# Graph layer on one core: node ranges of 46, ScalarE loads edge attributes, SyncE fetches part of the source rows

## What is computed

```python
nodes = node_state[edges].reshape(num_edges, -1)      # source's and destination's features: 128
gates = (ssp(edge_state @ We1 + be1) @ We2 + be2) * soft_cutoff(edges_distance)
h = ssp(nodes @ Wn1 + bn1) @ Wn2 + bn2
message_sum = zeros.at[edges[:, 1]].add(h * gates)     # scatter-add by destination
new_state = node_state + (ssp(message_sum @ Ws1 + bs1) @ Ws2 + bs2)
out = layernorm(x + new_state)
```

## Time and profile before

| | us |
|---|---|
| median of 3 runs | 2500.21 (2497.41 to 2500.76) |
| span of the profiled execution, first to last instruction | 1988.8 |
| median less span: what lies around the instructions | 511.4 |
| GpSimd (POOL) busy, 1572 instructions | 1484.7 (75%) |
| TensorE (PE) busy | 1737.7 (87%) |
| ScalarE (ACT) busy | 1532.1 (77%) |
| VectorE (DVE) busy | 1285.6 (65%) |
| mean granted TensorE clock | 0.949 of full speed |

### The profile page before, as it was taken

How to read it: one execution, slowest core, us unless ns; L and a number is a source line. 1 busy time by engine, 2 the same in 40 slices (tenths; PEclk the granted TensorE clock), 3 DMA queues, 4 the chain that set the end, 5 groups by cost and what they waited for, 6 DMA issues and landing times.

```text
span 1988.8 us, 53540 instructions
## 1 busy us (share of the span) xinstructions
PE 1737.7 (87%) x16249; PEld 1328.7 (67%) x16249; DVE 1285.6 (65%) x3512; ACT 1532.1 (77%) x3368; POOL 1484.7 (75%) x1572
## 2 busy tenths in 40 slices
PE   4699999898888988878889988998988898988987
PEld 3577777676666666666666766766666676766666
DVE  4578888666665655555656666666666666666666
ACT  3589999777777777777777788788777787787877
POOL 7777777777777777777777777777777777777773
PEclk7799999999999899999989999899999899999999
DMA  5433333333333333333333333333333233333331
GB/s 122 122 85 98 97 97 97 85 85 76 91 74 73 71 73 70 75 68 71 74 71 74 74 80 74 74 75 78 74 75 75 69 84 75 75 78 75 75 76 38
DMA packets 256432, 157.78 MB, mean 79 GB/s; under 512 B 45401, under 2 KB 227046, under 8 KB 256366
## 3 DMA queue, kind: packets, MB, share of 16 engines
q1 hardware_dynamic: 202652, 104.94, 18.2%
q0 software_dynamic: 50048, 51.35, 15.5%
q10 hardware_dynamic: 3666, 0.68, 0.2%
HBM read 146.94 MB, written 9.87 MB: 79 GB/s over the span
## 4 chain that ended last, share of the span: by engine, by line
POOL 57%; issue 22%; PE 11%; DVE 3%; ACT 2%; SPq 2%; DMA 2%; DVEq 1%; ACTq 1%; POOLq 0%
POOL ga L459 57%; PE ps L623 3%; PE ps L636 3%; PE ps L640 1%; DVE hid L1113 1%; SPq L340 1%; PE ps L585 1%; DMA ga<-in_x_dram,srcT 1%; PE ps L575 1%; DVE hid L1117 1%; PE ps L653 1%; PE ps L662 1%; PE ps L577 0%; DVEq L1139 0%; ACT lg L861 0%
## 5 line engine op out<-in xcount | busy, mean ns | idle before, releaser
L459 POOL DMA_INDIRECT ga<-in_x_dram,srcT x1564 | 1483.7, 949 | 477.6 <-issue 472.4
L852 ACT ACTIVATE lg<-ps,bn1c 128x512 f32<-128x512 f32 x391 | 268.4, 687 | 306.6 <-PE ps L585 267.6
L636 PE MATMUL ps<-wn,hid 128*128 128x64 f32 x3128 | 447.9, 288 | 18.9 <-DVE hid L1117 17.1
L1113 DVE SCALAR_TENSOR_TENSOR hid<-ps,neg_b,lg 128x512 f32<-128x512 f32 x391 | 292.8, 749 | 221.9 <-ACT lg L867 205.2
L636 PEld LDWEIGHTS ps<-wn,hid 128*128 128x128 f32 x3128 | 393.1, 197 | 51.5 <-DVE hid L1117 26.6
L575 PE MATMUL ps<-ident,ea 128*128 128x128 f32 x782 | 173.8, 305 | 198.2 <-DMA ga<-in_x_dram,srcT 135.2
L844 ACT COPY xe<-ps 128x512 f32<-128x512 f32 x391 | 229.9, 588 | 113.3 <-PE ps L577 99.8
L623 PE MATMUL ps<-xe,wn 64*128 64x256 f32 x1564 | 289.8, 449 | 0.0
L1151 DVE TENSOR_TENSOR acc<-acc,ps 64x64 f32 x782 | 168.4, 215 | 163.7 <-issue 157.9
L640 PE MATMUL ps<-we,hid 128*128 128x128 f32 x1564 | 273.1, 299 | 0.0
L575 PEld LDWEIGHTS ps<-ident,ea 128*128 128x128 f32 x782 | 80.0, 143 | 282.1 <-issue 268.8
(11 more groups left out here) (124 smaller groups left out, 1847.9 us busy)
## 6 DMA issues: line engine op xcount, KB each, us to landing
ea<-in_edge_attr_dram SPq DMA_DIRECT2D x195, 256.0 KB
ga<-in_x_dram,srcT POOLq DMA_INDIRECT x1564
bw<-b_tab SPq DMA_DIRECT2D x782, 32.0 KB
relb<-rel_tab SPq DMA_DIRECT2D x196, 64.0 KB
b_tab<-share SPq DMA_DIRECT2D x25, 250.0 KB
out_dram<-xs SPq DMA_DIRECT2D x25, 125.0 KB
xs<-in_x_dram SPq DMA_DIRECT2D x3, 750.0 KB
rows_i<-in_dst_dram SPq DMA_DIRECT2D x1, 768.0 KB
```

The costliest lines, as they stand in the source:

```text
L459: pool.indirect_dma_start(to[:, t % 2, t // 2, :], None, x, bass.IndirectOffsetOnAxis(ap=idx[:, t:t + 1], axis=0)).then_inc(done, 16)
L636: pe.matmul(hg[:, t * D:(t + 1) * D], hid[:, u % 2, t * P:(t + 1) * P], wn2[:, :], start=False, stop=False, skip_group_check=True)
L852: act.activation(lg[:, u % 2, 0:QUAD].rearrange("p (k e) -> p k e", k=2), z[:, :, 0:PAIR], ACT.Abs, bias=bn1c[:, 0:1]).then_inc(n_abs, 1)
L1113: dve.scalar_tensor_tensor(out=hid[:, u % 2, 0:QUAD].rearrange("p (k e) -> p k e", k=2), in0=ps[:, 2 * (u % 2):2 * (u % 2) + 2, 0:PAIR], s ...
```

## The change

1. `W` is 46. The layout in partitions stays at halves of 64 (`HALF`). `bw` loads have 46 rows, the one-hot of the scatter has 4 x 46 columns, its matmuls 46, the adds into `acc` 46.
2. A second table `wb_all` holds the places in bytes, so SyncE needs no arithmetic between reading a place and the `bw` load. ScalarE stores and loads that table at the start.
3. The loads of edge attributes are issued by ScalarE, after the bias refill of every other quad.
4. For 23 quads (32, 48, ..., 384) the last of the four gathers is gone. SyncE loads the 128 source rows of it one by one, each with a DMA of 256 B into `stage`: 16 of them in each two-quad step from 22 quads before (`load_rows`), their addresses read from `row_at`. In the step of four quads before, `hand_rows` copies the 128 rows to the `ga` buffer. GpSimd waits for that copy (`handed`) before its third gather of the quad.
5. `row_at` is filled before SyncE's first step with every second of 256 entries of `src` for 23 quads, 2944 words of 4 bytes on one partition; VectorE multiplies them by 256 after its step 7 (`row_ready`).
6. SyncE's loops are written out.

```diff
-W = 64
+HALF = 64
+W = 46
 RING = 4
 ARING = 16
 EPS = 1e-5
 SHARES = 2
 SOON = 2
 BRING = 8
+
+ROWS0 = 32
+ROWS_EVERY = 16
+ROWS_N = 23
+ROWS_BEFORE = 22
+ROWS_TURN = (16,) * 8
...
+        def issue_ea(eng, q, u):
+
+            if isinstance(q, int) and q == NQ - 1:
+                full = edge_attr[q * QUAD:q * QUAD + PAIR, :].rearrange("(p j) d -> p (j d)", j=2)
+                eng.dma_start(ea[:, u, 0, :], full).then_inc(s_ea[u], 16)
+                part = edge_attr[q * QUAD + PAIR:E, :].rearrange("(p j) d -> p (j d)", j=2)
+                eng.dma_start(ea[0:REMP // 2, u, 1, :], part).then_inc(s_ea[u], 16)
+            else:
+                two = edge_attr[bass.ds(q * QUAD, 2 * QUAD), :]
+                eng.dma_start(ea[:, u:u + 2, :, :].rearrange("p q k c -> p (q k) c"),
+                              two.rearrange("(m p j) d -> p m (j d)", p=P, j=2)).then_inc(s_ea[u], 16)
...
+            def load_rows(q):
+
+                i, turn = divmod(q - (ROWS0 - ROWS_BEFORE), ROWS_EVERY)
+                turn //= 2
+                if not (q >= ROWS0 - ROWS_BEFORE and i < ROWS_N):
+                    return
+                if i == 0 and turn == 0:
+                    sp.wait_ge(row_ready, 1)
+                if i >= 2 and turn == 0:
+                    sp.wait_ge(xe_t, ROW_QUADS[i - 2] + 1)
+                first, n = ROWS_FIRST[turn], ROWS_TURN[turn]
+                _, places = nc.values_load_multi_w_load_instructions(
+                    row_at[:, i * P + first:i * P + first + n], engines=(mybir.EngineType.SP,), min_val=0,
+                    max_val=(N - 1) * D * 4, skip_runtime_bounds_check_because=IN_X)
+                for r, place in enumerate(places):
+                    sp.dma_start(stage[first + r:first + r + 1, i % 2, :].bitcast(U8),
+                                 x_bytes[bass.ds(place, D * 4)].rearrange("(r b) -> r b", r=1)).then_inc(s_stage[i % 2], 16)
+
+            def hand_rows(q):
+
+                i = (q - (ROWS0 - 4)) // ROWS_EVERY
+                if (q - (ROWS0 - 4)) % ROWS_EVERY or not 0 <= i < ROWS_N:
+                    return
+                quad = ROW_QUADS[i]
+                sp.wait_ge(s_stage[i % 2], P * 16 * (i // 2 + 1))
+                sp.wait_ge(xe_t, quad - (ARING - 1))
+                sp.dma_start(ga[:, quad % ARING, 1, 1, :], stage[:, i % 2, :]).then_inc(handed, 16)
 
...
-                    w_all[0:1, bass.ds(q * 2, 2 * n)], engines=(mybir.EngineType.SP,), min_val=0, max_val=N - W,
+                    wb_all[0:1, bass.ds(q * 2, 2 * n)], engines=(mybir.EngineType.SP,), min_val=0, max_val=(N - W) * F * 4,
                     skip_runtime_bounds_check_because=IN_RANGE)
                 load_rel(q, u)
                 load_bw(q, v, firsts)
-                if reached(q, RING):
-                    load_ea(q, u)
+                load_rows(q)
+                hand_rows(q)
 
...
+                sp.wait_ge(row_e, XCOLS)
+                sp.dma_start(row_at.rearrange("p (i e) -> p i e", e=P),
+                             src[(ROWS0 + 1 - ROWS_EVERY) * QUAD:(ROW_QUADS[-1] + 1) * QUAD].rearrange(
+                                 "(a i e) -> a i e", a=1, e=ROWS_EVERY * QUAD)[:, :, (ROWS_EVERY - 1) * QUAD + PAIR + 1:ROWS_EVERY * QUAD:2]).then_inc(ld_row, 16)
...
+                ahead = NODE0 + STEPS
+                for q in range(BRING, NQ):
+                    stored, made, node = (q - 12) // 4, (q - 7) // 4, (q - (ahead + STEPS - 1)) // STEPS
+                    if q % 4 == 0 and 1 <= stored < NG:
+                        share_stored(stored // 2, stored % 2)
                     fast_step(q, q % BRING)
-                store_share(2, 0)
-                with sp.Fori(2, NG // 2 + 1) as i:
-                    for u in range(BRING):
-                        if u % 4 == 0:
-                            share_stored(i - (2 - u // 4), 1 - u // 4)
-                        fast_step(i * BRING + u, u)
-                        if u % 4 == 3:
-                            store_share(i * 2 - (1 - u // 4), 1 - u // 4)
-                for q in range((NG // 2 + 1) * BRING, (NG // 2 + 2) * BRING):
-                    if q % 4 == 0:
-                        share_stored(NG // 2 - 1 + q % BRING // 4, 1 - q % BRING // 4)
-                    fast_step(q, q % BRING)
-
-                ahead = NODE0 + STEPS
-                steps(sp, (NG // 2 + 2) * BRING, ahead, 0, BRING, fast_step)
-                with sp.Fori(0, EARLY - 1) as g:
-                    for u in range(STEPS):
-                        fast_step(g * STEPS + (ahead + u), (ahead + u) % BRING)
-                    store(g)
-                for q in range(TAIL0, NQ):
-                    fast_step(q, q % BRING)
-                    if q == TAIL0 + STEPS - 1:
-                        store(EARLY - 1)
-
+                    if q % 4 == 3 and SHARES <= made < NG:
+                        store_share(made, made % 2)
+                    if q % STEPS == (ahead - 1) % STEPS and 0 <= node < EARLY:
+                        store(node)
...
-                gather_rows(ga[:, q % ARING], srcT[:, 4 * q:4 * q + 4], s_ga[q % ARING])
+                to, idx, done = ga[:, q % ARING], srcT[:, 4 * q:4 * q + 4], s_ga[q % ARING]
+                if q in ROW_QUADS:
+
+                    gather(to, idx, 0, done)
+                    gather(to, idx, 1, done)
+                    pool.wait_ge(handed, 16 * (ROW_QUADS.index(q) + 1))
+                    gather(to, idx, 2, done, 32)
+                else:
+                    gather_rows(to, idx, done)
 
...
-                        weights, rows = (wn1[half, 0, :], xe[half, u, 1, :]) if end == 0 else (bw[half, b, :], ohT[half, u % 2, :])
+                        near = slice(k * HALF, k * HALF + W)
+                        weights, rows = (wn1[half, 0, :], xe[half, u, 1, :]) if end == 0 else (bw[near, b, :], ohT[near, u % 2, :])
                         pe.matmul(ps[:, 2 * (u % 2) + k, 0:PAIR], weights, rows,
...
+            act.wait_ge(wb_ready, 1)
+            act.dma_start(wb_tab.rearrange("a (g p c) -> p (a g) c", p=P, c=2), wb_i[:, :, :]).then_inc(wb_stored, 16)
...
+            act.wait_ge(wb_stored, 16)
+            act.dma_start(wb_all[:, :], wb_tab[:, 0:NQ * 2]).then_inc(w_loaded, 16)
...
+                if u % 2 == 1:
+                    issue_ea(act, q + RING + 1, (u + 1) % RING)
...
                 four_steps(1, 1, 0, False, True)
+                dve.wait_ge(ld_row, 16)
+                dve.tensor_scalar(row_at, row_at, float(D * 4), None, ALU.mult).then_inc(row_ready, 1)
                 with dve.Fori(1, NG // 2) as m:
```

More of the change, by code:

```diff
@@ L25 @@
 BRING = 8
+ROWS0 = 32
[3 more added lines that the diff above has]
+ROWS_TURN = (16,) * 8
+ROWS_FIRST = tuple(sum(ROWS_TURN[:n]) for n in range(len(ROWS_TURN)))
 IN_RANGE = "windows' places are the least of N - W and of destinations, which are nodes"
+IN_X = "sources are nodes"
 def reached(i, n):
@@ L85, in gnn_layer @@
     assert RG > 1 and RL > 1
+    ROW_QUADS = [ROWS0 + ROWS_EVERY * i for i in range(ROWS_N)]
+    assert sum(ROWS_TURN) == P and all(n % 4 == 0 for n in ROWS_TURN) and 2 * len(ROWS_TURN) == ROWS_EVERY
+    assert ROWS0 % 2 == 0 and ROWS0 >= ROWS_EVERY and ROW_QUADS[-1] < NQ - 4
     STEPS = 8
@@ L120, in gnn_layer @@
         w_tab = nc.dram_tensor("w_tab", (1, RG * P * 2), I32, kind="Internal").ap()
+        wb_tab = nc.dram_tensor("wb_tab", (1, RG * P * 2), I32, kind="Internal").ap()
+        x_bytes = x.rearrange("n d -> (n d)").bitcast(U8)
+        b_bytes = b_tab.rearrange("n f -> (n f)").bitcast(U8)
         ident = sb("ident", [P, P])
@@ L185, in gnn_layer @@
         bw = sb("bw", [P, BRING, F])
+        stage = sb("stage", [P, 2, D])
         relb = sb("relb", [P, RING, PAIR], U8)
@@ L201, in gnn_layer @@
         dst_i = rows_d[:, :, :].rearrange("p g e -> p (g e)")[:, 0:NT].bitcast(I32)
+        row_at = rows_i[0:1, :, :, :].rearrange("p a g e -> p (a g e)")[:, 0:ROWS_N * P]
         gen_flat = sb("gen_flat", [P, 10 * P])
@@ L260, in gnn_layer @@
         g_oh, g_mm, g_add = ([sem(f"{n}{k}") for k in range(2)] for n in ("g_oh", "g_mm", "g_add"))
+        ld_row, row_ready, wb_ready, wb_stored = (sem(n) for n in ("ld_row", "row_ready", "wb_ready", "wb_stored"))
+        handed = sem("handed")
+        s_stage = [sem(f"s_stage{k}") for k in range(2)]
         filled, hg_set = sem("filled"), sem("hg_set")
@@ L310, in load_ea @@
                     sp.wait_ge(xe_t, q - (RING - 2))
[L311 to L319, removed]
+                issue_ea(sp, q, u)
             def load_rel(q, u):
@@ L454, in _, with gather @@
             pool.iota(iota_pi[:, :], pattern=[[1, 1]], base=0, channel_multiplier=1).then_inc(iotas, 1)
+            def gather(to, idx, t, done, inc=16):
+                pool.indirect_dma_start(to[:, t % 2, t // 2, :], None, x,
+                                        bass.IndirectOffsetOnAxis(ap=idx[:, t:t + 1], axis=0)).then_inc(done, inc)
             def gather_rows(to, idx, done):
```

(5 more changed lines are left out.)

18 lines of the change are left out of this document (11 added, 7 removed).

## The result

The changed kernel takes 3599.2 us (median of 4 runs, 3586.1 to 3624.8) against 2498.8 us (4 runs), a ratio of 1.4395 with a 95% interval of 1.4349 to 1.4441. Forecast were 2522 us and at most 2620: the direction was right, the size off by 1077 us.

A forecast was written before the change was run, and what follows sets the result against it. GpSimd, issuing gathers without a stop, was taken as the bound. A new wait of 50.6 us less 28.8 us for 23 dropped gathers gave +21.8 us on 2500.2 us, so 2522 us, range 2487 to 2620.

The forecast's parts named there:

- the 511.4 us around it: Time outside the profiled span of 1988.8 us, left unchanged so that a difference carries over to the median of 2500.2 us.
- later hand-overs are in time: After quad 32, SyncE needs 78.4 us per 16 quads and GpSimd 79.0, so GpSimd has no later waits to speak of.
- waits at every 16th quad: Sign against the forecast: GpSimd waiting again at every 16th quad would mean SyncE is the bound.
- 23 gathers fewer: GpSimd's stream: 23 gathers at 1.254 us each dropped, a gain of 28.8 us.
- Load of `row_at`: SyncE's queue at the start: 2944 words delay the first products by 19 us, bounds 0 and 44.
- The rule of the Trainium skill that I set beside the row: `row_at` load drains on one DMA engine, as in the 19 us; over 16 engines it would cost under 2 us.
- `row_ready`: SyncE's first step with rows, quad 10, waits for VectorE's multiplication: 7 us, bounds 0 and 12.
- One-row DMA and the read of 16 registers: SyncE's two-quad step: 0.24 us for each one-row DMA, 1.3 us for each read of 16 registers.
- The step, 9.8 us: SyncE's work per two quads sums to 9.8 us, just within GpSimd's 9.87 us.
- The wait at quad 32: GpSimd waits 50.6 us before quad 32's third gather, for rows handed over after SyncE's step of quad 28.
- SyncE becomes the bound: Rival: from a step of 9.9 us SyncE sets the pace; a step of 10.4 gives +128 us, 2628. Chance 0.27.
- Edge attributes on ScalarE, nothing; ranges of 46, nothing: ScalarE's waits for TensorE cover its added loads; narrower ranges shorten TensorE and VectorE work, not the bound: both 0 us.

The follow-up runs named there:

- a lead of 4: The changed kernel with GpSimd held to 4 quads ahead of TensorE's transposes, not 16: 2727.7 us, 1.0782 of the kernel before (2534.0 us).

## Why the prediction missed

**The step that failed.** "All sums are against the profiled span of 1988.8 us; the 511.4 us around it I leave as they are." Nothing lies around a span but 2 us. The profile has the span of kind A (1988 to 1993 us there), the times are of kind B, where the span itself is 2506.0 us and GpSimd, 57% of my chain, is in it by name nowhere; its gathers stand behind waits that the profile can't name, and one of them is worth 1.21 us of a quad. The gap of 20% between the profile and the times was a second machine, not an overhead; each of my terms was taken from the wrong one. The second step that failed hangs on it: "From then on SyncE needs 78.4 us for 16 quads and GpSimd 79.0, so later hand-overs are in time." The first wait was 68.2 us for 50.6 forecast, and 22 more came, 1297.7 us in all. I had named waits at every 16th quad as a sign that SyncE is the bound; it holds 4% of this chain, so the sign came for another reason. That the kernel is slower was forecast, but on kind B most of the loss is of a mechanism that I did not have: there the direction was luck.

**The burst, in no term and no rival.** On B a long wait of GpSimd brings on the next one. In the kernel before, GpSimd waits for TensorE after every four gathers, which lets the increments through. My new wait of 68.2 us lets its ring of 16 quads run empty, so 57 gathers follow without a pause; for 80 us SyncE and TensorE creep, SyncE does two steps in place of eight, and so the next hand-over is as late as the first. After the burst SyncE's step of quad 34 starts at 360.25 and six steps of 10.7 us bring the next hand-over to 424.2: the loss renews itself 22 times. A period of 145.5 us stands where 16 quads of the kernel before take 16 x 6.10 = 97.6 on this kind: 47.9 us, 22 times, are 1054 of the 1100 us lost. On A the same wait, 64.4 us, does not renew itself, since SyncE goes on during the burst; the next is 9.1 us.

**My numbers against kind A,** the machine that they were made for. Forecast +21.8 us, measured +91.8 (2083.8 against 1992.0), inside the forecast range of -13 to +120.

- *23 gathers fewer:* -28.8 us, as forecast: one each 1.25 us still.
- *Load of `row_at`:* forecast 19 us, first product at 66. The `relb` DMA behind it is held for 18.7 us, and TensorE's first product starts at 64.9. The rule of the Trainium skill that I set beside the row (DMA: Bandwidth & Descriptors, "Why a DMA increments its semaphore by 16 and not by 1") fits: 18.7 us is near the 19 that it gave and far from the under 2 of 16 engines. On which engines the load ran is in no view, and the trace can't tell the moving of the words from the setting up of the load.

```profile
38.84 18.74 SPq L354
58.88 5.91 DMA bw<-b_tab
64.92 2.08 PE ps L677 x8
```

- *`row_ready`:* forecast 7 us, measured 10.9, within its bounds.
- *One-row DMA and the read of 16 registers:* forecast 0.24 and 1.3 us.

```profile
L381 SPq DMA_DIRECT2D stage<-in_x_dram x2944: 224/228/1281, 130.2 to 2008.0; - x197
...
L377 SPq TENSOR_LOAD <-rows_i x184: 1137/1231/1397, 129.0 to 2001.8; - x184
```

The Trainium skill (Runtime: NRT & Kernel Launch, "Instruction fetch mechanics") has about 200 ns a register; 1.231 us for 16 is 77 ns, and the measurement decides.

- *The step, 9.8 us:* mis-sized. The hand-overs of the first six row quads lie at 231.5 to 673.0 us, (673.0 - 231.5) / 40 = 11.0 us per step. The term is the four `bw` loads. Until 683 us and after it, by source line:

```profile
L363 SPq DMA_DIRECT2D bw<-b_tab x192: 238/386/2547, 156.5 to 676.3; - x192
```
```profile
L363 SPq DMA_DIRECT2D bw<-b_tab x512: 238/251/2495, 684.4 to 1952.2; - x171
```

I took 0.28 us for each; their mean is 0.58 between the hand-overs at 231.5 and 673.0 us (93.3 us for 160) and 0.355 between those at 673.0 and 1948.4 (182.0 for 512); four of them take 2.3 us in the first stretch, not 1.1: all of the missing 1.2 us. The first is about the stretch in which SyncE also stores the shares of `b_tab`; that the stores do it is not shown. After it the step is (1948.4 - 673.0) / 128 = 9.96 us, near my 9.8 and GpSimd's 9.87.

- *The wait at quad 32:* forecast 50.6, measured 64.4; *later waits:* forecast none, measured 128.7 - 64.4 = 64.3 us, 50 of them in the next five row quads. 128.7 - 28.8 = 99.9 us; GpSimd's last gather starts 2060.1 - 1962.2 = 97.9 us later. So of my cases "SyncE becomes the bound" (0.27) is what kind A shows, until 673 us.
- *Edge attributes on ScalarE, nothing; ranges of 46, nothing:* together they cost 2.3 to 2.6% on B, and how it splits is open. On A the ranges are right to 0.2% in time, but not in "TensorE and VectorE are not the bound": TensorE's busy time went from 1737.7 to 1840.6 us at a lower clock, and GpSimd hid it. The edge attributes on ScalarE were not run by themselves.
- *The range:* its upper end, 2620 us, was to stand for a step of 10.4 us, for which my own sum gave 2628. Nothing hangs on it.

**On kind B** the loss splits, by ratios of runs of one set each: 1.023 for ranges and ScalarE's loads, 1.08 with the row DMAs but without the wait (or with it and a lead of 4), 1.42 to 1.44 with the wait and the burst.

## What to carry to other kernels

Before reading any row, hold the profiled execution's span against the timed runs; where they differ by more than a few us, ask for the profile of such a run, since its bound may be another engine. A new wait on an engine with a deep ring is priced by what that engine does afterwards: it comes back with a whole ring of transfers to issue at once, and a ring no deeper than the latency needs limits that burst. Test a wait apart from the work that feeds it; here one constant separated 866 us from the rest.

## What the runs showed of the hardware

- The same program takes 1992 to 1993 us on two of these chips and 2506 to 2534 us on four others, steady to 1% on each. What differs, in the chips or beside the program, is not known.
- On the second kind, semaphore increments and instructions of TensorE, SyncE and, at the start, ScalarE are held back while GpSimd issues indirect DMAs back to back: 1.40 to 1.45 us of delay for each gather, which GpSimd issues every 1.25 us, so the delay outlasts a burst of 57 by 9 us. In it instructions of TensorE and SyncE come about 0.7 us apart or a multiple of it: three weight loads of L677 start at 284.17, 284.89 and 285.58 us, the matmuls above 2.8 us apart. That the gathers do it is shown by taking a gather out (1.21 us a quad) and by breaking up the burst (866 us); the path is inferred from times. The data itself does not lag: in the 9 us after the burst the DMA engines are busy for 0.02 of the time. Which path is full is not shown.
- TensorE's granted clock falls to 0.54 and 0.50 (the 1.2 GHz level) in these stretches, in which it is busy for 12 of 68 us, and stands at 0.50 for the first 8 us after them. Eight matmuls of L690 take 1.90 us there, at 365.19 us, and 1.03 at 372.64, so the recovery is slower for it.
- Ranges of 46 in place of 64 lower the granted clock, from 0.946 to 0.958 down to 0.879 to 0.900 on kind A, with as many matmuls; which of the narrower instructions does it is not shown.
